# Target one-hots of two gather rounds: eight scalar operations per group in place of tensor compare and product

## What is computed

```python
# layer 0
xw = x @ W;  ew = edge_attr @ edge_w
out = segment_sum(xw[src] * ew, dst) + b;            x = layernorm(x + out)
# layer 1
ht = einsum('ni,rio->nro', x, weight)
msg = ht[src, edge_types] * edge_norm[:, None]
out = relu(segment_sum(msg, dst) + bias);            x = layernorm(x + out)
# layer 2: edge weights by a small MLP on x[src], x[dst], normalised by degrees, segment sum
# layer 3: four times  x = relu((x + segment_sum(x[src], dst)) @ W1 + b1) @ W2 + b2
```

## Time and profile before

| | |
|---|---|
| Median of 3 runs | 4776.23 us (4770.1 to 4780.95) |
| Profiled execution, span from first to last instruction | 4768.7 us (7.5 below the median; no other time of it is given) |
| Busy: PE / PEld | 3392.9 us (71%) / 2236.1 us (47%) |
| Busy: DVE | 2341.6 us (49%), 5563 instructions |
| Busy: ACT | 1316.9 us (28%) |
| Busy: POOL | 2458.3 us (52%), 2489 instructions |
| Round 1 / 2 / 3 (gathers) | 81.6 to 1084.4 / 1138.2 to 2166.6 / 2211.0 to 3192.8 us |
| Mean granted TensorE clock | 0.831 of full speed |

### The profile page before, as it was taken

The page is one execution under the profiler, slowest core; times in us unless marked ns, Lnnn a source line. Parts: engine busy times, 40 slices in busy tenths (PEclk is TensorE's granted clock), DMA queues, the critical chain, the costliest instruction groups (busy, mean ns, idle before and its releaser), DMA issues.

```text
span 4768.7 us, 66594 instructions
## 1 busy us (share of the span) xinstructions
PE 3392.9 (71%) x22549; PEld 2236.1 (47%) x22549; DVE 2341.6 (49%) x5563; ACT 1316.9 (28%) x3113; POOL 2458.3 (52%) x2489
## 2 busy tenths in 40 slices
PE   3888888885676766774333333347777999999998
PEld 3554545553455544552222222236774555555554
DVE  6755555553566565663555555546773111111122
ACT  1233223322122222222444444436772000000000
POOL 3777777774777777775777777753230000000000
PEclk8999999997888888886555555558998999999999
DMA  3343344442333333334777777776776777777776
GB/s 106 105 125 120 121 134 133 130 124 94 91 99 95 99 103 100 99 90 115 197 199 200 200 200 199 197 207 231 267 264 245 279 276 281 280 277 280 291 295 224
DMA packets 506525, 855.10 MB, mean 179 GB/s; under 512 B 111339, under 2 KB 284439, under 8 KB 506180
## 3 DMA queue, kind: packets, MB, share of 16 engines
q1 hardware_dynamic: 338752, 542.03, 32.4%
q0 software_dynamic: 87808, 179.98, 14.9%
q10 hardware_dynamic: 79620, 128.70, 7.5%
HBM read 632.93 MB, written 217.55 MB: 178 GB/s over the span
## 4 chain that ended last, share of the span: by engine, by line
POOL 48%; PE 27%; issue 16%; DVE 4%; ACT 3%; DMA 1%; SPq 0%; DVEq 0%; ACTq 0%; POOLq 0%
POOL big L767 33%; POOL big L794 16%; PE psS L1774 11%; PE psA L1774 11%; ACT big L1143 2%; PE psS L1451 2%; PE ps L1720 1%; PE ps L1711 1%; DVE xn L2363 1%; PE psA L1655 1%; DVE wcol L2367 1%; DMA big<-in_src_dram 0%; PE ps L1644 0%; DMA big<-A_rows 0%; PE ps L1386 0%
## 5 line engine op out<-in xcount | busy, mean ns | idle before, releaser
L767 POOL DMA_INDIRECT big<-ht_rows,reli x784 | 790.7, 1009 | 275.4 <-issue 238.6
L767 POOL DMA_INDIRECT big<-xw_rows,srci x784 | 765.1, 976 | 308.7 <-issue 238.7
L794 POOL DMA_INDIRECT big<-axt_rows,srci x784 | 744.3, 949 | 264.1 <-issue 238.5
L1451 PE MATMUL psS<-big 128*128 128x128 f32 x3136 | 505.4, 329 | 310.6 <-DMA big<-ht_rows,reli 309.5
L1451 PEld LDWEIGHTS psS<-big 128*128 128x128 f32 x3136 | 473.8, 239 | 381.0 <-DMA big<-ht_rows,reli 346.7
L851 POOL TENSOR_TENSOR xsb<-xsb,l3b2r 128x896 f32<-128x896 f32 x6 | 12.5, 2078 | 1115.1 <-DMA xsb<-x_keep 1115.1
L1774 PE MATMUL psS<-big,xsb 128*128 128x448 f16 x1372 | 484.9, 353 | 18.6 <-DMA big<-A_rows 18.6
L1596 PE MATMUL ps<-identh,xsb 128*128 128x128 bf16 x784 | 101.4, 311 | 546.4 <-DVE xsb L2266 546.4
L1774 PE MATMUL psA<-big,xsb 128*128 128x448 f16 x1372 | 484.7, 353 | 0.0
L1774 PE MATMUL psS<-big,acc 128*128 128x448 f16 x1372 | 483.6, 352 | 0.0
L1774 PE MATMUL psA<-big,acc 128*128 128x448 f16 x1372 | 483.6, 352 | 0.0
(11 more groups left out here) (291 smaller groups left out, 5129.9 us busy)
## 6 DMA issues: line engine op xcount, KB each, us to landing
big<-A_rows SPq DMA_DIRECT2D x112, 2744.0 KB, 13.5
A_rows<-xsb ACTq DMA_DIRECT2D x196, 416.0 KB, 2.7
xg_rows<-big SPq DMA_DIRECT2D x98, 512.0 KB, 3.8
big<-xg_rows SPq DMA_DIRECT2D x98, 512.0 KB, 3.7
marks_rows<-big SPq DMA_DIRECT2D x98, 354.0 KB
big<-marks_rows SPq DMA_DIRECT2D x98, 354.0 KB, 4.6
big<-srcq_list SPq DMA_DIRECT2D x98, 256.0 KB
ht_rows<-big ACTq DMA_DIRECT2D x28, 512.0 KB
```

The source lines that it names most:

```text
L767: pool.indirect_dma_start(ring[g % len(ring)][:, j * D:(j + 1) * D], None, table[:, :], bass.IndirectOffsetOnAxis(ap=lists[:, g * TPG + j: ...
L794: pool.indirect_dma_start(wide[g % NS][:, j, :], None, axt_rows[:, :], bass.IndirectOffsetOnAxis(ap=srci[:, g * TPG + j:g * TPG + j + 1], ...
L1451: m = pe.matmul(psS[b][:, 0:P], rows[b][:, j * P:(j + 1) * P], marks[b][:, j * P:(j + 1) * P], start=(j == 0), stop=(j == TPG - 1))
```

## The change

`make_onehots` makes eight scalar operations of 128 x 128 instead of one tensor operation of 128 x 1024. Each takes the targets of its tile as a scalar per partition. Where weights are given (round 2), the weight column is the second scalar of the same instruction, and the separate product goes, with the semaphore pair `r_ohraw` and the counts handed in for it. Round 3 has its own code and is unchanged. Lines behind the deleted ones move up by one to five.

```diff
-        r_ohraw = sem2("r_ohraw")
...
-            def compare(b, base, w, it):
-                return dve.tensor_tensor(tiles(onehot[:, b, :]), iota[:, window(base, w)].unsqueeze(1).broadcast_to([P, TPG, P]),
-                                         columns(dstf, it, b), ALU.is_equal)
-
-            def make_onehots(b, base, w, it, raw_count, weights):
-                if weights is None:
-                    compare(b, base, w, it).then_inc(r_oh[b], 1)
-                else:
-                    compare(b, base, w, it).then_inc(r_ohraw[b], 1)
-                    dve.wait_ge(r_ohraw[b], raw_count + 1)
-                    dve.tensor_tensor(tiles(onehot[:, b, :]), tiles(onehot[:, b, :]), columns(weights, it, b),
-                                      ALU.mult).then_inc(r_oh[b], 1)
+            def make_onehots(b, base, w, it, weights):
+                for j in range(TPG):
+                    to, numbers = onehot[:, b, j * P:(j + 1) * P], iota[:, window(base, w)]
+                    if weights is None:
+                        m = dve.tensor_scalar(to, numbers, column(dstf, it, b, j), None, ALU.is_equal)
+                    else:
+                        m = dve.tensor_scalar(to, numbers, column(dstf, it, b, j), column(weights, it, b, j),
+                                              ALU.is_equal, ALU.mult)
+                m.then_inc(r_oh[b], 1)
...
-                    make_onehots(b, bases[g], 0, it, it + R.w0, weights)
+                    make_onehots(b, bases[g], 0, it, weights)
```

More of the change, by code:

```diff
@@ L2055, in finish @@
                             with dve.Fori(1, more + 1) as w:
-                                make_onehots(b, base, w, pair, pair * nwin + w, weights)
+                                make_onehots(b, base, w, pair, weights)
                                 add_sums(b, base, w, q + w, q)
@@ L2060, in ring_round @@
                         pair = it * HALFB + n // 2
-                        make_onehots(b, load_base(pair, b), 0, pair, pair * nwin, weights)
+                        make_onehots(b, load_base(pair, b), 0, pair, weights)
                         if n0 is not None:
@@ L2099, in round_ @@
                     q = (l * NIT + it + R.g0) * nwin
-                    qw = (it + R.w0) * nwin
                     for b in range(2):
@@ L2104, in round_ @@
                         bases.append(load_base(it, b))
-                        make_onehots(b, bases[b], 0, it, qw, weights)
+                        make_onehots(b, bases[b], 0, it, weights)
                     for b in range(2):
@@ L2109, in round_ @@
                             with dve.Fori(1, more + 1) as w:
-                                make_onehots(b, bases[b], w, it, qw + w, weights)
+                                make_onehots(b, bases[b], w, it, weights)
                                 add_sums(b, bases[b], w, q + w, q)
```

## The result

The changed kernel takes **4813.2 us** (median of 4 runs, 4807.0 to 4833.6), the one before 4775.0 (4 runs, 4770.1 to 4781.0): ratio 1.0084, 95% interval 1.006 to 1.0107, **0.8% slower**. Forecast were 4717 us, 1.2% faster. Its profiled execution took 4818.8 us, with a span of 4816.9, 48.2 us above that of before; so it lies a little above the median, and that difference is larger than the 38 us between the medians.

A forecast was written before the change was run, and what follows sets the result against it. GpSimd's gathers, one after the other, were taken as the bound. -22.2 + 3.6 us in round 1, -45.0 + 3.6 in round 2 and + 0.4 at the start gave -59.6 from 4776.2: 4717 us, range 4703 to 4742.

The forecast's parts named there:

- What bounds the kernel: Rounds 1 to 3: each lasts as long as GpSimd's 784 gathers one after the other; GpSimd waits for no engine.
- The comparison's stretches go: Rounds 1 and 2: removing the tensor comparison ends its holds on gathers, 22.2 us in round 1, 45.0 in round 2.
- What the scalar operations do to the gathers: New one-hot trains, rounds 1 and 2: 137 starts at 0.026 us, 3.6 us a round; ends 0 and 19 us.
- Rival (b): New train of eight hands over without a gap, holding one gather per group to its end: 4903 us, chance 0.03.
- Rival (c): Tensor operations aren't the cause of the held gathers, and scalar ones add 19 us a round: 4814 us, chance 0.02.
- VectorE's cost: One-hots on VectorE: 51 us more busy time in round 1, 69 less in round 2, beside its waiting, costing nothing.
- The first message: Start of round 1: the sixth group's gathers wait for the first group's later message, about 0.4 us, once.

The follow-up runs named there:

- round2_only: The changed kernel with the tensor comparison of the kernel before kept in round 1, scalar operations in round 2 only; 4806.3 us, ratio 1.0065 to the kernel before.
- break_all: The changed kernel with nine tiny one-input reduces per group between the ten wide scalar operations; 4723.5 us, ratio 0.9894 to the kernel before.
- f32_both: The changed kernel with L2028 and L2031 both reading the f32 node numbers in place of the f16 table; 4993.5 us, ratio 1.0451 to the kernel before.

## Why the prediction was wrong, by its steps

- *What bounds the kernel.* Right. GpSimd still waits for nothing but "issue" and the start; the gathers are 41 us longer in all, and from first to last start the two rounds are 42 us longer.
- *The comparison's stretches go.* Right: the one-hots hold no gather for over 0.12 us in rounds 1 and 2, and with the trains broken the kernel comes to 4723.5, 7 us from the forecast.
- *What the scalar operations do to the gathers* is **the step that failed.** I priced the new train alone, 0.026 us a start from L2266, 3.6 us a round. That price was right: starts in L2000 and L2002 that aren't locked out carry 3.4 and 2.5 us. But I took L2032 and L2035 as harmless, since these "trains of five, hold none by more than 0.09". That was read in a trace in which the comparison stood ahead of them in every group. A row can show what an operation does in its present company only; I removed the company and kept the row. The term put at nothing is 28.7 + 72.1 = 101 us of lockouts in L2028 and L2031, against the 67 us saved. The upper end of the term, 19 us a round for starts that wait for one operation each, was no bound, since the lock outlasts the operation.
- *Rival (b)*, a train that hands over without a gap, is the mechanism, with 0.03. It was put on the new train instead of the old one, and priced at one catch per group; 49 of 196 groups had one. Its deciding point, 0.34 us a group, was sound: the lockouts cost 101 / 196 = 0.51. *Rival (c)* gave 4814, 1 us from the measured time, by luck: the tensor operations did hold the gathers. Where the comparison still stands, in round 1 of `round2_only`, starts in it carry 25.5 us; where it is gone and the trains are broken (`break_all`), the kernel is 51 us faster than before.
- *The Trainium skill's rule* (SBUF — State Buffer, Who interferes with whom) is that scalar operations in a two-port mode lock GpSimd out of descriptor generation. I set it aside on the strength of the trace. The runs bear out that scalar operations do hold gathers, wide ones above all; no run shows the mode they ran in. The rule says that the lock lasts for the instruction; the 49 lockouts last to the end of the train, up to 2.42 us over. Its other half, that tensor_tensor does not stall DMA, no run bears out: the earlier trace rows.
- *VectorE's cost.* 51 us more in round 1 as forecast (604 to 655 us between 80 and 1105 us), off the path. In round 2 the saving was 29 us (240 to 211, the one-hots alone) in place of 69, as the second scalar costs 56 ns an operation; the prediction took nothing and allowed for 218 more. Off the path as well.
- *The first message.* GpSimd stands idle for 1.48 us, 1.2 more than the usual 0.30, not 0.4:

```profile
131.66 1.20 DVE L2086 TENSOR_TENSOR big<-big,ps 128x1024 f32<-128x1024 f32 x1
...
133.13 0.94 POOL L766 DMA_INDIRECT big<-xw_rows,srci  x1 [1.48 <-DVE big L2086]
```

The product L2086 starts 1.13 us later than before (131.66 in place of 130.53), 0.52 of which the one-hots account for, and the gather starts 0.27 us after its end. Small, and in the right place.

## What to carry to other kernels

Where GpSimd's gathers are the path, every VectorE operation that can hold a gather is on the path too, and a train of them can hold one gather for as long as the train lasts. Look for trains of wide scalar operations that meet gathers. Where a trace shows gathers that end with the last of a train, break it with a small operation of one input: that was worth 1.9% in the changed kernel, and cost 0.4% in the kernel before, where nothing was locked out. When removing an operation, don't take the harmlessness of its neighbours from a trace in which it still stands.

## What the runs showed of the hardware

- A gather has two points at which it can be held: 0.13 us after its start (it then ends 0.82 us after the release) and 0.12 us before its end. A tensor operation with two SBUF inputs holds it at the first alone, scalar trains at either.
- A gather that meets a train of wide scalar operations is either let in within 0.2 us (16-bit operations of 512 columns) or 0.4 us (f32), or it waits for the end of the train: up to 2.4 us over with ten 16-bit operations, 3.6 us with ten f32 ones. With small reduces in between it gets in at the first one.
- Requests at nearly the same place of a train come out both ways: of the gathers whose first request falls 0.155 to 0.225 us after the start of the first L2028, 16 are locked out in rounds 1 and 2 and two are not. All 49 lockouts of the changed kernel fall in trains that VectorE starts without idle time, 56 of the 60 in `f32_both`; but in the kernel before, 298 gathers meet such trains and none is locked out. What decides stays open.
